# Quantised cross attention: two of seven row tiles turned by DMA, sums and clips on GpSimd, V roundings on VectorE

## What is computed

```python
def _fq(x, delta, zp, n_bits):
    xi = _round_ste(x / delta) + zp
    xq = jnp.clip(xi, 0.0, 2.0 ** n_bits - 1.0)
    return (xq - zp) * delta

sim = jnp.einsum('bhid,bhjd->bhij', _fq(q, dq, 128.0, 8), _fq(k, dk, 128.0, 8)) * SCALE
attn = jax.nn.softmax(sim, axis=-1)
out = jnp.einsum('bhij,bhjd->bhid', _fq(attn, dw, 0.0, 8), _fq(v, dv, 128.0, 8))
```

## Time and profile before

| what | value |
|---|---|
| median of 3 runs | 2426.47 us (2419.76 to 2426.48) |
| the profiled execution | 2418.64 us, of which the trace spans 2417.0 us |
| mean granted TensorE clock | 0.907 of full speed |
| busy over the span | PE 82%, DVE 71%, ACT 56%, POOL 29% |
| the stage of the change | about 1683 to 2353 us of the span |

### The profile page before, as it was taken

The page is one execution under the profiler, slowest core; times in us unless marked ns, Lnnn a source line. Parts: engine busy times, 40 slices in busy tenths (PEclk is TensorE's granted clock), DMA queues, the critical chain, the costliest instruction groups (busy, mean ns, idle before and its releaser), DMA issues. The chain is left out here.

```text
span 2417.0 us, 58085 instructions
## 1 busy us (share of the span) xinstructions
PE 1986.4 (82%) x19941; PEld 1285.8 (53%) x19941; DVE 1709.3 (71%) x3300; ACT 1360.2 (56%) x2415; POOL 694.8 (29%) x510
## 2 busy tenths in 40 slices
PE   3778677599999999999887785445988888888888
PEld 3778243266666666666534452222555555555553
DVE  3556496677777777777523326995899999999984
ACT  2544243266666666666533333222888888888862
POOL 0000161111111111111000002331766666666630
PEclk8999798799999999999988897556999999999999
DMA  7888000223323323233009980000111111111100
GB/s 193 228 237 222 5 1 0 77 71 91 91 68 95 84 75 95 79 80 95 20 38 280 270 228 1 0 0 26 42 40 35 38 38 38 38 38 38 38 1 15
DMA packets 108285, 190.36 MB, mean 79 GB/s; under 512 B 19886, under 2 KB 75294, under 8 KB 108222
## 3 DMA queue, kind: packets, MB, share of 16 engines
q1 hardware_dynamic: 103614, 164.95, 25.2%
q0 software_dynamic: 4608, 24.58, 3.1%
HBM read 127.13 MB, written 25.49 MB: 63 GB/s over the span
## 5 line engine op out<-in xcount | busy, mean ns | idle before, releaser
L1217 DVE TENSOR_REDUCE c_part<-c_mxp 128x1 f32<-128x500 f32 x672 | 429.4, 674 | 173.7 <-PE c_mxp L1106 169.3
L1190 ACT ACTIVATE c_e<-c_stp 125x896 f32<-125x896 f32 x384 | 351.9, 917 | 97.1 <-PE c_stp L1118 96.5
L1854 ACT ACTIVATE c_e<-c_sp,alpha 128x750 f32<-128x750 f32 x448 | 392.7, 882 | 23.6 <-PE c_sp L1798 21.4
L1812 PE MATMUL c_tp<-ident_h,c_ph 128*128 128x128 f16 x2688 | 230.5, 223 | 72.7 <-DVE c_pt L1874 70.8
L1812 PEld LDWEIGHTS c_tp<-ident_h,c_ph 128*128 128x128 f16 x2688 | 181.1, 100 | 167.7 <-DVE c_pt L1874 113.5
L1106 PE MATMUL c_mxp<-c_kh,c_qb 128*128 128x500 f16 x672 | 254.2, 380 | 3.1 <-DVE c_part L1217 2.2
L1874 DVE TENSOR_SCALAR c_pt<-c_tp 125x768 bf16<-125x768 f16 x448 | 246.3, 550 | 3.5 <-PE c_tp L1812 2.2
L1768 POOL TENSOR_SCALAR c_ki<-c_clipped 128x500 bf16<-128x500 bf16 x96 | 193.0, 2010 | 150.6 <-DVE c_clipped L1885 138.3
L1060 POOL TENSOR_TENSOR c_qs<-qst,mask_quad_ 96x224 f16<-96x224 f32 (+1 forms) x128 | 67.5, 556 | 578.1 <-PE c_stp L1118 578.1
L1133 PE MATMUL c_pvp<-c_e,c_vx 125*32 125x168 f32 (+1 forms) x6144 | 227.0, 265 | 0.6 <-ACT c_e L1190 0.4
L1918 DVE TENSOR_SCALAR c_ph<-c_e,c_inv 128x1500 f16<-128x1500 f32 x224 | 224.1, 1000 | 4.3
(11 more groups left out here) (267 smaller groups left out, 3452.9 us busy)
## 6 DMA issues: line engine op xcount, KB each, us to landing
c_ct<-ctx_turned SPq DMA_DIRECT2D x64, 750.0 KB
ctx_turned<-l_ct POOLq DMA_DIRECT2D x32, 750.0 KB, 4.7
c_ks<-c_kh SPq DMA_DIRECT2D x256, 93.8 KB
f_ct<-ctx_turned SPq DMA_DIRECT2D x32, 750.0 KB
l_cn<-in_ctx SPq DMA_DIRECT2D x32, 672.0 KB
f_cn<-in_ctx SPq DMA_DIRECT2D x32, 672.0 KB
c_ks<-c_kl SPq DMA_DIRECT2D x128, 93.8 KB
l_cn<-in_ctx SPq DMA_DIRECT2D x32, 78.0 KB
```

Source lines behind the costliest of these rows:

```text
L1190: act.activation(e[:, j % 4, :].rearrange("p (a c) -> p a c", a=2), stp[0:KP, 2 * (j % 2):2 * (j % 2) + 2, 0:448], ACT.Exp, scale=SCALE).t ...
L1217: dve.reduce_max(part[:, s // 3, s % 3:s % 3 + 1], mxp[:, (PIECES * p + s) % 2, 0:500], axis=AX.X).then_inc(piece_max, 1)
L1812: last = pe.transpose(tp[:, h, 128 * k:128 * k + 128], ph[r][:, KP * j:KP * j + 128], m.ident_h[:, :])
L1854: act.activation(e[r][:, HALF * h:HALF * h + HALF].rearrange("p (k c) -> p k c", k=2), sp_[:, 2 * h:2 * h + 2, 0:375], ACT.Exp, scale=m.al ...
```

## The change

Five things change inside `quantised_cross_attention`; nothing else in the program does.

1. Of each item, row tiles 1 and 4 are turned by a DMA transpose issued from SP, the other five by TensorE as before. For the two, VectorE makes an extra pass (`pc`: clip at 255 and take the offset away, f16 to bf16, 128x1500). Pieces of V and of the weights are 128 tokens wide instead of 125, with the last one padded by zeros.
2. The totals of the row sums go from VectorE to GpSimd.
3. Both clips of a projection go to GpSimd, each of two operations: one f32 to f32 (min, max), one f32 to bf16 (add, mult). VectorE's clip is gone.
4. The roundings of V (three of six) go from ScalarE to VectorE, reading PSUM.
5. The order moves: weights of tile t are made one slot later (slot t+1) with four buffers of `e` instead of two; projections are in slots 0, 1, 2, 4, 5, 6; `weigh` runs in slots 3 and 5, six pieces each.

```diff
+        PROJECT = (0, 1, 2, 4, 5, 6)
+        WEIGH = {3: (0, 6), 5: (6, NJ)}
+        E_BUFFERS = 4
+        ON_VECTOR = (3, 4, 5)
+        BY_DMA = (1, 4)
...
+                        for k, t in enumerate(BY_DMA):
+                            wait_apart(sp, p_clipped, ND * a + k + 1, beat)
+                            sp.dma_start_transpose(pt[p][:, :, 128 * t:128 * t + 128], pc[k][:, :]
+                                                   ).then_inc(dma_turned[k], 16)
...
+                def clip(n, p, k, live):
...
+                    wait_apart(pool, proj_rounded, i + 1, beat)
+                    pool.tensor_scalar(clamped[k % 2][0:rows, 0:width], rounded[k % 2][0:rows, 0:width],
+                                       ROUND + 127.0, ROUND - 128.0, ALU.min, ALU.max).then_inc(proj_clamped, 1)
...
+                    pool.tensor_scalar(out, clamped[k % 2][0:rows, 0:width], -ROUND, 1.0, ALU.add, ALU.mult
+                                       ).then_inc(proj_ready, 1)
...
+                    for t in range(NT):
+                        if live(1):
+                            i = NT * (n - 1) + t
+                            wait_apart(pool, exped, 2 * i + 2, beat)
+                            pool.tensor_scalar(total[:, t:t + 1], half[:, t, 0:1], half[:, t, 1:2], m.delta[:, 7:8],
+                                               ALU.add, ALU.mult).then_inc(totalled, 1)
+                        if live(0) and t in PROJECT:
+                            clip(n, p, PROJECT.index(t), live)
...
                 def weigh(a, p, j, first):
                     if j == 0:
-                        pe.wait_ge(p_copied, 2 * NT * (a + 1))
+                        pe.wait_ge(p_copied, 2 * NP * (a + 1))
+                        for k in range(ND):
+                            pe.wait_ge(dma_turned[k], 16 * a + 16)
...
+                def invert(a, t):
+                    i = NT * a + t
+                    dve.wait_ge(totalled, i + 1)
+                    dve.reciprocal(inv[:, t:t + 1], total[:, t:t + 1]).then_inc(inverted, 1)
...
+                    dve.tensor_scalar(ph[r][:, 0:NK], e[t % E_BUFFERS][:, :], inv[:, t:t + 1], HALF_ROUND,
+                                      ALU.mult, ALU.add).then_inc(p_ready, 1)
+                    if t in BY_DMA:
+                        k = BY_DMA.index(t)
+                        dve.wait_ge(p_ready, i + 1)
+                        if not first:
+                            dve.wait_ge(dma_turned[k], 16 * a)
+                        dve.tensor_scalar(pc[k][:, 0:NK], ph[r][:, 0:NK], HALF_ROUND + 255.0, HALF_ROUND, ALU.min,
+                                          ALU.subtract).then_inc(p_clipped, 1)
...
+                                if t - 2 in BY_PE:
+                                    copy_turned(n - 1, 1 - p, t - 2, h)
+                            if h == 0 and made:
+                                invert(*item)
+                        if made:
+                            weights(*item, r, first)
+                        if live(0) and t in PROJECT and PROJECT.index(t) in ON_VECTOR:
+                            k = PROJECT.index(t)
+                            i = 6 * n + k
+                            dve.wait_ge(proj_done, i + 1)
+                            dve.wait_ge(proj_clamped, i - 1)
+                            dve.tensor_scalar(rounded[k % 2][0:128, :], pp[0:128, 0:512], m.rdelta[0:128, 6:7],
+                                              ROUND, ALU.mult, ALU.add).then_inc(proj_rounded, 1)
```

More of the change, by code:

```diff
@@ L1705, in quantised_cross_attention @@
         pair = lambda name, shape, d=F32: [sb(f"{name}{p}", shape, d) for p in range(2)]
[L1706 removed]
+        W = 128 * NJ
         HALF = NK // 2
[L1708 to L1709 removed]
+        PROJECT = (0, 1, 2, 4, 5, 6)
[3 more added lines that the diff above has]
+        BY_DMA = (1, 4)
+        BY_PE = [t for t in range(NT) if t not in BY_DMA]
+        ND, NP = len(BY_DMA), len(BY_PE)
+        USED_BACK = [4 if t >= E_BUFFERS else NT if t == 3 else 3 for t in range(NT)]
+        ct = pair("ct", [128, W])
         ki = pair("ki", [128, NK], BF16)
[L1711 removed]
+        vi = pair("vi", [128, NJ, D], BF16)
         rounded = pair("rounded", [128, 512])
[L1713 removed]
+        clamped = pair("clamped", [128, 512])
         qb = pair("qb", [128, HQ], BF16)
[L1715 removed]
+        e = [sb(f"e{t}", [128, NK]) for t in range(E_BUFFERS)]
         ph = pair("ph", [128, W], F16)
[L1717 to L1719 removed]
+        pc = [sb(f"pc{k}", [128, W], BF16) for k in range(ND)]
+        half = sb("half", [128, NT, 2])
+        total, inv = sb("total", [128, NT]), sb("inv", [128, NT])
+        pt = pair("pt", [128, NJ, HQ], BF16)
         masked = sb("masked", [128, 4, NQ])
@@ L1770, in _ @@
-                sweep(pool, step, 0)
+                    pool.memset(ct[p][:, NK:W], 0.0).then_inc(set_once, 1)
+                for k in range(ND):
+                    pool.memset(pc[k][:, NK:W], 0.0).then_inc(set_once, 1)
+                def clip(n, p, k, live):
+                    i = 6 * n + k
+                    rows, width = (128, 500) if k < 3 else (128, 512)
+                    if k >= 2 or live(1):
+                        pool.wait_ge(proj_ready, i - 1)
+                    wait_apart(pool, proj_rounded, i + 1, beat)
+                    pool.tensor_scalar(clamped[k % 2][0:rows, 0:width], rounded[k % 2][0:rows, 0:width],
+                                       ROUND + 127.0, ROUND - 128.0, ALU.min, ALU.max).then_inc(proj_clamped, 1)
+                    if k < 3 and live(2):
+                        pool.wait_ge(s_done, 2 * NT * (n - 1))
+                    if k >= 3 and live(2):
+                        pool.wait_ge(weighed, NJ * (n - 2) + 4 * (k - 2))
+                    wait_apart(pool, proj_clamped, i + 1, beat)
+                    out = (ki[p][:, 500 * k:500 * k + 500] if k < 3 else
+                           vi[p][:, 4 * (k - 3):4 * (k - 3) + 4, :].rearrange("p j c -> p (j c)"))
+                    pool.tensor_scalar(out, clamped[k % 2][0:rows, 0:width], -ROUND, 1.0, ALU.add, ALU.mult
+                                       ).then_inc(proj_ready, 1)
@@ L1807, in turn @@
                         pe.wait_ge(p_ready, NT * a + t + 1)
-                    if not (first and t == 0):
-                        pe.wait_ge(p_copied, 2 * (NT * a + t) + h - 1)
+                    if not (first and t == BY_PE[0]):
+                        pe.wait_ge(p_copied, 2 * (NP * a + BY_PE.index(t)) + h - 1)
                     for k in range(6):
                         j = 6 * h + k
-                        last = pe.transpose(tp[:, h, 128 * k:128 * k + 128], ph[r][:, KP * j:KP * j + 128],
+                        last = pe.transpose(tp[:, h, 128 * k:128 * k + 128], ph[r][:, 128 * j:128 * j + 128],
                                             m.ident_h[:, :])
```

149 lines of the change are left out of this document (68 added, 81 removed).

## The result

The changed kernel takes 2469.05 us, the median of 4 runs (2462.66 to 2479.3), beside 2423.11 us for the kernel before on the same chip (4 runs, 2419.2 to 2426.48). The ratio is 1.0194, 95% interval 1.0153 to 1.0235: slower by 1.9%. The forecast was 2410.5 us and faster, so its sign was wrong. The range of 2350 to 2490 holds the time only because it takes in a rival: the spread of the query in front of tile 6's weights (2452 to 2482).

The account below looks back on a forecast made before the run. VectorE was taken to bound most of the stage, TensorE the V slots. Step 20.47 to 19.6 + 0.25 saves 0.62 us, times 31 is 19, less 3 for the ends: 16 us saved, 2410.5 us; range 2350 to 2490.

Parts of the forecast that it names:

- the spread of the query in front of tile 6's weights: Rival: GpSimd's query spread takes ports before tile 6's weights, VectorE stands up to 1.4 us; 2452 to 2482 us; chance 0.26.
- 18.5 floor: VectorE's step without lock waits: 16.4 us of work plus 2.1 us of bare waits for turns.
- bubbles between weights and copy: VectorE waits for TensorE's turn before copying; 0.69 us each, bare for tiles 6, 0 and 2, 2.1 us per step.
- three V roundings, start to start: VectorE rounds V from PSUM, 0.61 us each from start to start, 1.8 us per step.
- lock behind clips: Nine VectorE passes per step sometimes find GpSimd's clips holding the shared ports; 0.8 us of waiting per step.
- lock behind the spread: GpSimd's 1.68 us query spread no longer hits a total on VectorE; priced at 0.3 us per step (nothing to 1.5).
- half clock: TensorE's clock dip after its slot 1 wait costs 0.51 us per step before; half, 0.25 us, was kept.
- The prediction's own sign of being wrong: Among its signs of error: weights in slot 0 taking 2 us and more.
- The waits eat the gain: Rival: 0.5 us more waiting per step makes it a draw at 2426 us, within 7 us; chance 0.12.
- the rival of 1.45 us: Rival: GpSimd's f32 clip costs what its bf16 clip does, so the lock bounds at 25.0 us per step; 2569 us; chance 0.09.
- Transposes late: Rival: DMA transposes take 20 us each, TensorE waits 7 us at slot 3 every step; +220 us; chance 0.03.
- Half clock for good: Rival: TensorE stays at half clock, its 16 us of work needing over 30; +300 us; chance 0.02.

Follow-up runs that it names:

- narrow spread: Changed kernel, but from the third item on GpSimd spreads the query over 2 of 16 heads: 2408.68 us, ratio 0.9951 to the kernel before.
- short spread: The kernel before the change, with the query spread over 2 of 16 heads from the third item on: 2376.29 us, ratio 0.9809.
- e3_all_by_pe: Changed kernel without DMA transposes, all seven tiles turned by TensorE: 2503.22 us, ratio 1.0337 to the kernel before.
- e4_v_on_scalar: Changed kernel with the roundings of V back on ScalarE: 2400.78 us, ratio 0.9908 to the kernel before.
- e5_spread_slot3: Changed kernel with the whole query spread moved behind the total of slot 3: 2421.73 us, ratio 1.0005 to the kernel before.
- e6_scalar_slot3: Changed kernel with V roundings back on ScalarE and the whole query spread in slot 3: 2375.56 us, ratio 0.9827 to the kernel before.
- e11_totals_back: e6_scalar_slot3 with the totals back on VectorE: 2507.9 us, ratio 1.0353 to the kernel before.
- the spread in halves: Changed kernel with V roundings on ScalarE, weights before copies, and the spread as 8 heads each in slots 3 and 4: 2354.13 us, ratio 0.9709.
- e10_three_dma: e6_scalar_slot3 with three tiles (0, 2, 4) turned by DMA instead of two: 2410.85 us, ratio 0.9966 to the kernel before.
- e2_weights_first: Changed kernel with VectorE making reciprocal and weights before the copies: 2444.24 us, ratio 1.0102 to the kernel before.

## Why the prediction was wrong

The step was forecast at 19.85 us (18.5 floor, 1.1 lock, 0.25 clock) and measured at 22.18. By its own terms, per step:

| term | forecast | measured | from |
|---|---|---|---|
| bubbles between weights and copy | 2.1 | 2.07 | narrow spread, at full clock |
| three V roundings, start to start | 1.8 | 2.1 | timeline of the changed kernel: 0.77, 0.65, 0.66 |
| reciprocal between two copies, five times | 0.35 | 0.8 | timeline: 0.18 in four of five, 0.07 in one |
| extra pass, each of two | 0.55 | 0.57 | group |
| lock behind clips | 0.8 | 0.9 | weights of tiles 0 to 5 |
| lock behind the spread | 0.3 | 1.1 | weights of tile 6; narrow spread |
| half clock | 0.25 | 1.0 | tiles 0 and 1; narrow spread |

The excesses add up to 2.4 us; 2.33 were to be explained. Two thirds are the last two rows.

**The step that failed is the price of the spread,** "for it I take 0.3 (nothing to 1.5)". It is not a mean over random meetings. The order repeats in every step: the third V rounding ends, two clips of 0.6 us run, the spread starts, and 0.45 or 0.32 us later VectorE wants the ports. I had written just this down in the rival, and gave it 0.26 because a clip of another length might shift the order. With my own clip of 0.65 us, placing the events from the end of the last rounding on would have put the spread in front: two clips at some 0.8 us from start to start put the spread after 1.7 to 1.9 us, and mask, reduction, two copies and a reciprocal put the weights after 2.1 us. The prediction's own sign of being wrong, weights of 2 us in slot 0, is what the trace shows. The loss by the clock is the other half of the same failure: I took the dip as a thing that gets rarer because "the wait of slot 1 gets shorter"; with 1.1 us of lock in front of it, that wait grew to 2.34 us (1.21 before), and the dip came in every step instead of every third.

**What the forecast rested on.** In my ledger the kernel before had 1.3 us of lock and 0.51 of clock, the one after 0.3 and 0.25. Take both away from both: 20.47 - 1.3 - 0.51 = 18.66 before (measured with the short spread: 18.68) against 18.5 + 0.8 = 19.3 after (measured 19.92). Without the stall the ledger itself said slower. The forecast gain was a stall that I let vanish, and the question whether it vanishes got one sentence. That the range held the time is owed to the rival in it and not to the forecast's mechanism.

**The parts.** Sorted by runs: the DMA turns bring 34 us (undone alone, e3_all_by_pe); the V roundings on VectorE cost 68 (undone alone, e4_v_on_scalar), 2.1 us of work, less a hidden bubble, and the releases of clips right in front of weights. With the spread in slot 3 the same roundings cost 46 us (e5_spread_slot3 against e6_scalar_slot3), so a third of the 68 came through the spread. Whether the totals on GpSimd are worth having is not isolated (e11_totals_back moves the spread too). They have a price in this order: any total behind the spread is 1.25 us late in e4_v_on_scalar. The change put a good part and a bad part together. These prices aren't additive, since each of them moves the spread too.

**The rivals.** "The waits eat the gain" (2426) is not it, the loss is clear of it. The spread of the query is, with its time (2452 to 2482) and its condition: more than 1.7 us of waiting per step, measured 0.9 + 1.1, and the clock's 1.0 on top. It was right by the slot and by the lock, and it had the clock too low (0.5). Its upper end has a slip: 18.5 + 2.0 + 1.4 + 0.5 is 22.4 and not 22.2, so 2489 and not 2482. GpSimd's f32 passes alone took 0.60 to 0.62 us (forecast 0.65), so the rival of 1.45 us is excluded; the Trainium skill (GPSIMD Engine Reference, section 3.1) with its 769 ns for 512 elements is above what this trace shows. Transposes late: in the stage's list of waits TensorE waits for no transpose. In the packet records of the DMA queue a tile's 384 KB move in 1.55 us, beginning some 1.3 us after the extra pass; the estimate by the Trainium skill (Advanced Engine Details and Errata, X-Bar Transpose) was 1.1. Half clock for good: not seen.

What stays open: how the 4.5 us per step of e11_totals_back divide, what three DMA tiles are worth with the spread in halves, and whether the totals would be better placed ahead of the clips of their slot. None of these was tried.

## What to carry to other kernels

Where two engines share a lock, an average share of its time prices only what falls at random; in a loop that repeats, write the order of events down to tenths of a microsecond and see who is first, once for each long instruction. A stall that the kernel before has must be shown to leave before its price is counted as a gain: compute both ledgers without it first, and look at the sign. Here a long instruction that can't be avoided was better in two halves, in slots where the other engine has slack.

## What was unexpected in the hardware

- The lock goes both ways: who issues first holds it. In the changed kernel weights behind the spread took 2.10 us in the mean of 27 meetings, behind a second clip 1.27 (49), behind a first clip 1.20 (64), with nothing in front 0.99 (83). The Trainium skill (SBUF — State Buffer, Who interferes with whom) says that whoever issues first gets the shared ports for the whole instruction; the trace agrees but for some 0.2 us: the weights of 2111.98 end 0.79 us after the spread, where they need 0.99 alone.
- A 128x1 total on GpSimd, 0.34 us alone, obeys the same lock: 0.74 us in the mean of the stage. A tiny operation in a queue with a lock is not cheap.

```profile
2113.20 1.02 POOL L1805 TENSOR_SCALAR c_total<-c_half,delta 128x1 f32<-128x1 f32 x1
```

- GpSimd clips from f32 in 0.61 us for 512 elements what took it 1.45 us for 500 from bf16: two f32 passes cost less than the one before, by 0.2 us of busy time.
- Single waits of TensorE went with the half clock. The versions with a wait of more than 2.1 us in every step all show it: the changed kernel (2.34 and 2.36 us), e10_three_dma (2.16) and e11_totals_back (2.83), each at 0.92 from 1800 to 2300 us, and e3_all_by_pe (2.3; 0.95). With longest waits of 1.3 us (e1_narrow_spread, e5_spread_slot3), 1.5 (e2_weights_first) and 1.7 (e4_v_on_scalar) the clock was 1.00.
- The length of one wait is not the whole of it. The kernel before has waits of 1.0 and 1.2 us in every step and fell to half in one step of three. Behind the 2.34 us the half clock lasts from the turn of 2114.15 until the scores of 2117.55, which take 0.49 us again; behind the 2.36 us it begins only with the projection, 1.0 us after TensorE has gone on. In the changed kernel the half clock costs 1.0 us per step and the lock that brings it 1.1.
